# Cross attention on one Trainium2 core: in every step the product with the values two steps back is put ahead of the scores

## The reference

```python
hidden = jnp.concatenate([context, latents], axis=1)      # 1601 + 256 = 1857 keys
q = (latents @ Wq.T).reshape(b, q_len, H, HD)             # H = 16 heads of HD = 96
k = (hidden @ Wk.T).reshape(b, s_len, KV, HD)             # KV = 4 key/value heads
v = (hidden @ Wv.T).reshape(b, s_len, KV, HD)
...
scores = jnp.einsum('bkgqd,bksd->bkgqs', q, k) * scale
attn = jax.nn.softmax(scores.astype(jnp.float32), axis=-1).astype(q.dtype)
out = jnp.einsum('bkgqs,bksd->bkgqd', attn, v)
...
return out @ Wo.T
```

## Time and profile before

| | |
|---|---|
| time, median of 3 runs | 1926.09 us (1922.92 to 1926.54) |
| time of the profiled execution | 1923.49 us |
| its span | 1921.7 us |
| TensorE busy | 1871.0 us, 97% of the span |
| VectorE / ScalarE / GpSimd busy | 1233.9 / 1175.2 / 681.4 us (64%, 61%, 35%) |
| granted TensorE clock, mean | 0.994 |
| line 1152, values | 1440 matmuls, 376.1 us busy |
| line 1139, scores | 1440 matmuls, 374.6 us busy |
| line 1110, max | 512 matmuls, 152.8 us busy |
| the four attention parts | 811.9 to 1005.1 us of the span is that of batch 0; the others are alike |

### The profile page before, as it was taken

The page is one execution under the profiler, slowest core; times in us unless marked ns, Lnnn a source line. Parts: engine busy times, 40 slices in busy tenths (PEclk is TensorE's granted clock), DMA queues, the critical chain, the costliest instruction groups (busy, mean ns, idle before and its releaser), DMA issues. The chain is left out here.

```text
span 1921.7 us, 28060 instructions
## 1 busy us (share of the span) xinstructions
PE 1871.0 (97%) x9512; PEld 1538.3 (80%) x9512; DVE 1233.9 (64%) x2123; ACT 1175.2 (61%) x2067; POOL 681.4 (35%) x696
## 2 busy tenths in 40 slices
PE   7999999999999999999999999999999999999798
PEld 5888888888888788877779877788777797777576
DVE  5656656566566712578865688745788656887654
ACT  6666656666566633467775577764677755777620
POOL 5666757667576522112103012121121030110331
PEclk9999999999999999999999999999999999999899
DMA  4000101001010354200102001111001023000220
GB/s 171 28 28 28 49 15 45 27 27 44 11 55 13 114 193 128 56 5 17 28 20 72 19 9 28 28 39 56 5 17 28 20 72 139 9 17 9 90 83 28
DMA packets 59577, 89.86 MB, mean 47 GB/s; under 512 B 7252, under 2 KB 42452, under 8 KB 58710
## 3 DMA queue, kind: packets, MB, share of 16 engines
q1 hardware_dynamic: 59480, 88.57, 14.6%
HBM read 67.52 MB, written 21.03 MB: 46 GB/s over the span
## 5 line engine op out<-in xcount | busy, mean ns | idle before, releaser
L1152 PE MATMUL b_o_ps<-b_pr,b_v 128*97 128x512 f32 (+1 forms) x1440 | 376.1, 394 | 5.0 <-DVE b_pr L999 4.2
L1139 PE MATMUL b_s<-b_q,b_kt 97*128 97x512 f32 (+1 forms) x1440 | 374.6, 394 | 0.0
L1260 DVE TENSOR_REDUCE b_mx<-b_m 128x1 f32<-128x1024 f32 (+1 forms) x256 | 286.8, 1120 | 110.4 <-PE b_m L1110 109.6
L999 DVE TENSOR_TENSOR b_pr<-b_pf,b_pr 128x1024 fp32r<-128x1024 f32 (+1 forms) x256 | 314.6, 1229 | 65.3 <-ACT b_pr L993 65.1
L1211 ACT ACTIVATE b_pf<-b_s 128x1024 f32<-128x1024 f32 (+1 forms) x256 | 247.9, 968 | 127.9 <-PE b_s L1139 127.3
L1152 PEld LDWEIGHTS b_o_ps<-b_pr,b_v 128*97 128x97 f32 (+1 forms) x1440 | 232.1, 162 | 103.9 <-issue 12.2
L1308 POOL TENSOR_TENSOR b_y<-b_recs,b_o 96x512 f32<-96x512 f32 x32 | 41.3, 1291 | 769.1 <-ACT b_recs L1226 769.1
L1139 PEld LDWEIGHTS b_s<-b_q,b_kt 97*128 97x128 f32 (+1 forms) x1440 | 262.8, 185 | 61.8 <-issue 0.8
L993 ACT ACTIVATE b_pr<-b_pf 128x1024 fp32r<-128x1024 f32 (+1 forms) x256 | 257.7, 1007 | 48.3 <-PE b_o_ps L1152 44.6
L445 PE MATMUL a_ring<-a_xt,w_a 128*128 128x512 f32 x1128 | 276.8, 396 | 0.0
L445 PEld LDWEIGHTS a_ring<-a_xt,w_a 128*128 128x128 f32 x1128 | 207.2, 189 | 40.5
(11 more groups left out here) (119 smaller groups left out, 2594.4 us busy)
## 6 DMA issues: line engine op xcount, KB each, us to landing
hraw<-in_ctx_t SPq DMA_DIRECT2D x92, 128.0 KB, 2.4
raw_a<-in_w_qkv SPq DMA_DIRECT2D x30, 384.0 KB, 3.3
raw_a<-in_w_o SPq DMA_DIRECT2D x32, 256.0 KB, 3.1
queries<-a_q SPq DMA_DIRECT2D x24, 256.0 KB, 2.0
b_qraw<-queries SPq DMA_DIRECT2D x16, 384.0 KB, 3.9
attended<-b_y SPq DMA_DIRECT2D x32, 192.0 KB, 2.1
c_yraw<-attended SPq DMA_DIRECT2D x3, 1536.0 KB, 7.0
x_t<-a_xt SPq DMA_DIRECT2D x2, 2048.0 KB, 8.3
```

What stands on the lines that cost most here:

```text
L999: dve.tensor_tensor(pr[0:rows, k % 2, LO, 0:n], pf[0:rows, k % 2, 0:n], f(pr[0:rows, k % 2, HI, 0:n]), ALU.subtract).then_inc(p_lo.sem, 1)
L1139: mm = pe.matmul(ps_s[k % 2][0:rows, i * BANK:(i + 1) * BANK], kt[:, a, kv, t0:t0 + rows], q[:, kv % 2, m, hp * BANK:(hp + 1) * BANK], sta ...
L1152: mm = pe.matmul(ps_o[0:HD2 + 1, :], v[0:rows, a, t, g // 2, :], pr[0:rows, k % 2, m, i * BANK:(i + 1) * BANK], start=t == 0 and s == 0, s ...
L1260: dve.reduce_max(mx[:, g % 2, t, half:half + 1], ps_m[:, 0:MAXW[half][1]], X).then_inc(mx_made.sem, 1)
```

## The change

One line of `attention_steps`. Until now only the first step of a group had the values ahead of the scores; now each step has:

```diff
         step = [("scores", k)] + [("pv", k - 2)] * (k >= 2)
-        s += step if j else step[::-1]
+        s += step[::-1]
         if more and j == PAIRS - 1:
```

## The result

The changed kernel takes 2047.96 us (median of 4 runs, 2041.46 to 2051.15) against 1926.32 (4 runs, 1922.92 to 1928.16): **1.0628 times the time before, 95% interval 1.0606 to 1.065**, 121.6 us slower. The forecast was 2038, with a range of 1998 to 2066. The profiled execution took 2049.93 us, its span is 2048.1, 126.4 more than before, at a mean granted clock of 0.988.

The account below looks back on a forecast made before the run. TensorE sets the pace; the change takes the chain's slack. Stalls of 85.7 (groups 1 to 6), 6.2 (group 0) and 20.5 (last groups) sum to 112.4 us: profiled 1923.5 becomes 2036, median forecast 2038, range 1998 to 2066.

Parts of the forecast that it names:

- a chain of 5.14 us: One step, start of scores to its values, through exp, high and low parts: 5.14 us, handoffs of 0.44 included.
- the rival at 1985: Handoffs between engines hide behind TensorE's early weight loading, so the chain is 4.70 us; time about 1985; chance 0.09.
- no change: Chain under 4.9 us, with copy, sums and spread off it; time 1926; chance 0.03.
- faster: The buffer b_pr is the bound and its waits go; at most 5 us come back, 1921; chance 0.03.
- values(0), copy: Groups 1 to 6, first step: output copy stands ahead of the high part and delays values; stall 1.30 us.
- values(3), sums: Groups 1 to 6, step 3: low part stands behind max reduction and sums on VectorE; stall 0.97 us.
- values(4), spread: Groups 1 to 6, step 4: two spread copies before the high part, GpSimd's product beside low; stall 0.66 us.
- values(6), groups 1 to 5: Step 6: TensorE work of 4.62 us between scores and values against a chain of 5.14; stall 0.52 us.
- values(7): Last half step of a group: half a block's chain and a row ahead of it, so no stall.
- last group of batch 0: Last group of a batch, no max to fill: stalls 5.34 less 0.21 idle already there, 5.13 us.
- the upper bound: GpSimd's query copies stretch four low parts a batch, 9 us more; last values may add a little.
- the clock falls too: TensorE's idling in the attention stage halves the clock for a tenth of it; some 70 us more, about 2110; chance 0.05.

## Why the prediction was right, and where it was off

**The bound and the chain** were right. TensorE was the only bound; the change made it wait for a chain of 5.14 us, measured as 5.11, handoffs included. Had the durations alone counted (the rival at 1985), the chains of 5.11 above would read 4.7. One reading of the prediction was loose: of its 0.44 us between durations and chain, 0.16 is the tail of the scores' last matmul beyond the pace of 1.39. By the profile's own end of the block (935.79 + 1.55) only 0.04 lie between the scores and exp. The chain is the same either way. The rival at 1985 fell, and so did "no change" and "faster": the waits for `b_pr` went away, as the last one supposed, and gave nothing.

**The terms, stall by stall.** A stalled block also lasts 1.44 instead of 1.39 until the next, which the prediction had in its handoff of 0.18; it is added here.

| place | predicted us | measured us |
|---|---|---|
| values(0), copy | 1.30 | 1.24 + 0.04 |
| values(2) | 0.12 | 0.09 + 0.04 |
| values(3), sums | 0.97 | 0.93 + 0.04 |
| values(4), spread | 0.66 | 0.60 + 0.04 |
| values(6), groups 1 to 5 | 0.52 | 0.49 + 0.04 |
| values(6), group 6 | 0.52 | 1.01 + 0.04 |
| values(7) | 0 | 0.62 + 0.04 in two groups of a batch |
| group 0, whole | 1.55 | 26.35 - 24.80 = 1.55 |
| groups 1 to 6 of batch 0 | 21.4 | 170.31 - 148.60 = 21.7 |
| last group of batch 0 | 5.13 | 26.36 - 19.90 = 6.46 |

**A hit that is in part luck.** That the groups 1 to 6 grew by 21.7 us where 21.4 were forecast rests on two errors of one size. The sum adds its stalls to the time before, but in four of these six groups of batch 0 the kernel before already stalled at values(6), by 0.4 us. These waits went with the old order, and with the longer blocks 4 x 0.45 = 1.8 us should have come off, as the 0.21 of the last group did. Against it, two things were not in the sum. Values(6) of group 6 stand in the last group, where no max lies ahead of them: 1.01 instead of 0.52. And values(7) stall in two groups of a batch, where GpSimd splits the next queries while VectorE does low(7). VectorE, then GpSimd:

```profile
870.14 2.87 DVE L999 TENSOR_TENSOR b_pr<-b_pf,b_pr 65x512 fp32r<-65x512 f32 x1
...
870.06 2.40 POOL L1317 TENSOR_TENSOR b_q<-b_qraw,b_q 96x1024 fp32r<-96x1024 f32 x1
```

This low part of half the columns takes 2.87 us instead of 0.68, and values(7) stall by 0.61 to 0.64: 8 x 0.66 = 5.3 us in the kernel, inside the 9 that the upper bound set aside for GpSimd. Both together are 0.5 + 1.3 = 1.8 us a batch.

**What was missed** explains the 14 us between the sum, 112.4, and the 126.4 by which the span grew. I take it from where blocks start. From the first scores of a batch to those of the next 263.5, 264.4 and 264.4 us lay before, and 293.4, 293.6 and 294.1 lie now: 88.8 more for three batches. From the first scores of batch 3 to its last values it was 194.9 and is 227.4: 32.5 more. The first scores come 4.3 later, and the end is 0.8 further off. Together 126.4. Of these, the groups 0 are 6.3 (forecast 6.2), the groups 1 to 6 are 87.3 (85.7), and the last groups with what follows them 27.7 (20.5). So the misses lie in the last group and outside the attention.

- *The clock, about 8.* The rival "the clock falls too" had the mechanism right and its size tenfold too large, and I had dismissed it whole. In each batch's last group the clock drops for a few us. The changed kernel's timeline:

```profile
1011.36 1.60 PE L1152 MATMUL b_o_ps<-b_pr,b_v 128*97 128x512 f32 x6 [0.85 <-DVE b_pr L999]
...
1018.21 2.24 PE L1152 MATMUL b_o_ps<-b_pr,b_v 128*97 128x512 f32 x6 [1.77 <-issue]
1020.25 2.51 PE L1139 MATMUL b_s<-b_q,b_kt 97*128 97x512 f32 x6
1022.60 1.57 PE L1152 MATMUL b_o_ps<-b_pr,b_v 128*97 128x512 f32 x6
```

  The block of values takes 2.04 (1018.21 to 1020.25) instead of 1.43, the scores behind it 2.35 instead of 1.39: 1.6 us in each of the four batches, and in batch 3 a second time, behind the stall of 2.07 us.

- *The last values of batch 3, about 0.8.* I wrote that values(6) are covered by the projections that stand ahead. Batch 3 has no projections behind it. There, the changed kernel and then the kernel before:

```profile
1923.27 2.29 PE L1152 MATMUL b_o_ps<-b_pr,b_v 128*97 128x512 f32 x9 [1.28 <-DVE b_pr L999]
```

```profile
1797.68 2.30 PE L1152 MATMUL b_o_ps<-b_pr,b_v 128*97 128x512 f32 x9 [0.46 <-DVE b_pr L999]
```

  Against these two stands that the last groups came out some 0.4 us a batch short of the forecast otherwise, in part because their stalls are 1.94, 0.94 and 2.24 for 1.98, 0.97 and 2.39.

- *Ahead of the attention 4.3, behind the last values 0.8*, which no step of the change explains. The changed kernel's granted clock has two short drops in self-attention that the profiled execution of the kernel before hasn't. The other traces say that this is variation between executions: the kernel with copy and spread moved has the changed order but neither of the two drops, and its first scores start at 811.0, earlier than the 811.9 of the kernel before; in the one with the copy alone moved both stand, and the scores start at 816.6, beside 816.1 in the changed kernel. Behind the last values, the changed kernel took 123.4 us in one execution and 122.5 in another, where the kernel before took 122.6.

**What the changed profile was to show.** TensorE's share is 93%, not 92, since its busy time grew by 41 us. Some 8 of that are the slowed blocks, and more than half of it is a matter of the modelled ends: between blocks that follow each other the tail of a matmul lies under the next one, and ahead of each stall some 0.16 us of it shows as busy. In groups 1 to 6 of batch 0 that makes 153.23 - 147.59 = 5.6 us over some 30 stalls, at a clock of 1.00. For the same reason the waits read 90.8 us and not above 100: 125 stalls x 0.16 are the 20 us between idle time and stall (values(0): 1.24 and 1.08). The pace of two steps of 1024 columns, 6.5, was no sign at all: values(1) between them do not stall (849.59 to 852.86 is 3.27 for one step), and two such steps without a stall take 6.5 too. The steps with 834 columns do tell. The scores of two such steps of group 0, which has no helpers, start 6.56 apart in the changed kernel, where two steps took 6.33 before:

```profile
829.38 1.55 PE L1139 MATMUL b_s<-b_q,b_kt 97*128 97x512 f32 x6
...
835.94 1.56 PE L1139 MATMUL b_s<-b_q,b_kt 97*128 97x512 f32 x6
```

The attention part of batch 0 grew from 193 to 223 us, for 221. The longest stalls, at values(0) and values(4) of the last group, are 1.94 and 2.24 for 2.0 and 2.4. My sentence that nearly nothing of the wait ends at another engine than low holds by the times, but more than a third of it stands in the profile as "issue".

## What to carry to other kernels

Before a product is moved ahead of the work that covers its inputs, add up the chain of one step with its handoffs, and the work between its ends, for each step by itself. What counts is the smallest slack, and helpers that ride in the same queues (a copy, a reciprocal, a spread) decide where it is. Here 0.1 to 2.2 us were missing at most of the steps, and a block of 1.39 us moved by one place cost 6% of the whole. A queue that runs in order pays each stall in full, so an order that looks equal by count of instructions has to be followed through every queue that the moved entry feeds. A cheap test of how near a kernel is to such an edge is to lengthen the chain by a known piece: 0.33 us more cost 11 us in the old order and 42 in the new. And when a sum of stalls is added to a measured time, take off the waits that this time already holds.

## What was not expected of the hardware

**Short idles can take the clock down.** No stall of the attention is longer than 2.3 us. Still, windows of the changed kernel around the drop shown above read:

```profile
1010.00:1018.20 8.20, 5.59 (x27) 3.86 (x25) 3.13 (x3) 5.58 (x8) 0.00 (x0) 1.00 0.00 0
1018.20:1026.30 8.10, 7.35 (x24) 5.22 (x25) 2.55 (x3) 3.44 (x4) 0.00 (x0) 0.79 0.00 0
```

TensorE was busy 5.59 of 8.20 us with two idles of 0.85 and 1.77, and the clock behind them is 0.79 on the mean, a mixture of its two levels, 1.2 and 2.4 GHz. In the feed of the last layer it was busy 5.73 of 7.00 and kept 1.00. With the second idle filled to 0.38 the clock holds at this place in all four batches; it falls later, behind the stall of 2.08, in two of them. A stall of this length does not always bring the drop: in the kernel with the steps 0 to 4 reversed the idle of 1.77 stands in each batch, and in batch 1 the block behind it takes 1.44. The Trainium skill ("TensorE: Matmul & The Clock Gate", A second HAM failure mode: psum-queue depth-cycling) tells of a kernel whose clock swings because TensorE idles briefly between its groups of matmuls; this trace agrees in kind, with some 8 us for a time of 2048.

The runs agree with that. The changed kernel took 2041.46 at a mean clock of 0.993, 2045.99 at 0.991, 2049.93 and 2051.15 at 0.988. Its spread of 10 us, about twice that of the kernel before, goes with the clock: how many of the drops happen differs from execution to execution. Why, these runs don't show.
